# Attention with 32-row bands per head: one 1024-column exponential per key tile, and row maxima in three single PSUM banks

## The reference

```python
def _L0_xattn_ref(queries, keys, values, Wq, bq, Wk, bk, Wv, bv, Wo, bo):   # 8 heads of 4 columns
    q = _split_heads(queries @ Wq + bq)
    k = _split_heads(keys @ Wk + bk)
    v = _split_heads(values @ Wv + bv)
    scale = 1.0 / np.sqrt(D_MODEL / NUM_HEADS)
    attn = jax.nn.softmax(jnp.einsum('bhqd,bhkd->bhqk', q, k) * scale, axis=-1)
    o = jnp.einsum('bhqk,bhkd->bhqd', attn, v)
    return o.transpose(0, 2, 1, 3).reshape(b, s, h * hd) @ Wo + bo
...
x = x + jnp.tanh(g_xattn[0]) * _L0_xattn_ref(_layernorm(x), ctx_1024, ctx_1024, ...)
x = x + jnp.tanh(g_ffn[0]) * _L0_ffn_ref(_layernorm(x), ...)
```

## Time and profile before

| | |
|---|---|
| median of three runs | 595.02 us |
| the profiled execution | 594.75 us |
| its span | 592.9 us |
| PE, DVE, ACT, POOL busy | 551.4, 444.1, 397.4, 196.8 us |
| granted clock of TensorE | 1.00 until 500 us, 0.97 behind it |

### The profile page before, as it was taken

The page is one execution under the profiler, slowest core; times in us unless marked ns, Lnnn a source line. Parts: engine busy times, 40 slices in busy tenths (PEclk is TensorE's granted clock), DMA queues, the critical chain, the costliest instruction groups (busy, mean ns, idle before and its releaser), DMA issues.

```text
span 592.9 us, 12821 instructions
## 1 busy us (share of the span) xinstructions
PE 551.4 (93%) x5043; PEld 318.6 (54%) x5043; DVE 444.1 (75%) x811; ACT 397.4 (67%) x774; POOL 196.8 (33%) x193
## 2 busy tenths in 40 slices
PE   6798899998999989999999998899999999999994
PEld 4433333333333333333333344469889898898974
DVE  3889879996798967989897258746767868677541
ACT  2587789987888878898888830044665646655651
POOL 3058030024420063400158010240735626346234
PEclk9999999999999999999999999999999999999998
DMA  8600000000000000000000004122735556356133
GB/s 280 241 2 1 1 1 3 2 1 38 2 36 2 2 37 1 37 2 1 37 38 2 36 19 140 34 60 72 163 112 117 144 136 148 108 107 163 16 36 35
DMA packets 23807, 35.80 MB, mean 60 GB/s; under 512 B 3459, under 2 KB 16196, under 8 KB 23620
## 3 DMA queue, kind: packets, MB, share of 16 engines
q1 hardware_dynamic: 17604, 26.59, 13.8%
q0 software_dynamic: 6144, 8.39, 8.3%
HBM read 26.59 MB, written 8.39 MB: 59 GB/s over the span
## 4 chain that ended last, share of the span: by engine, by line
PE 67%; DVE 18%; ACT 5%; issue 4%; POOL 3%; DMA 1%; POOLq 0%; ACTq 0%; DVEq 0%; SPq 0%
PE ps L1719 15%; PE ps L1726 15%; PE ps L1488 12%; DVE mquart L1016 11%; PE ps L1475 6%; PE ps L1454 6%; PE ps L1384 2%; ACT probs L741 2%; PE ps L1345 2%; POOL xn L528 2%; PE ps L1360 1%; PE ps L1697 1%; PE ps L1672 1%; ACT osb L641 1%; PE ps L1513 1%
## 5 line engine op out<-in xcount | busy, mean ns | idle before, releaser
L1016 DVE TENSOR_REDUCE mquart<-ps 128x2 f32<-128x802 f32 x256 | 241.9, 988 | 33.4 <-PE ps L1454 30.2
L741 ACT ACTIVATE probs<-ps 128x512 f32<-128x512 f32 (+1 forms) x416 | 222.9, 599 | 24.0 <-PE ps L1475 20.8
L1488 PE MATMUL ps<-probs,vp 128*32 128x256 f32 (+1 forms) x1664 | 132.7, 391 | 4.5 <-ACT osb L641 4.5
L1454 PE MATMUL ps<-kpad,qrows 64*128 64x401 bf16 x512 | 90.6, 337 | 3.7 <-DVE mquart L1016 3.1
L1475 PE MATMUL ps<-qfull,kpad 64*128 64x256 bf16 (+1 forms) x832 | 89.8, 272 | 2.8 <-ACT x L762 0.9
L1313 DVE TENSOR_TENSOR h1l<-hf,h1h 128x512 fp32r<-128x512 f32 x64 | 44.4, 693 | 56.0 <-ACT hf L868 56.0
L867 ACT ACTIVATE h1h<-ps,b1T 128x512 fp32r<-128x512 f32 x64 | 44.0, 687 | 53.8 <-PE ps L1719 53.6
L1726 PE MATMUL ps<-w2h,h1h 128*128 128x256 f32 x256 | 73.8, 288 | 2.2 <-DVE h1l L1313 1.5
L1726 PE MATMUL ps<-w2l,h1h 128*128 128x256 f32 x256 | 72.4, 283 | 0.0
L1726 PE MATMUL ps<-w2h,h1l 128*128 128x256 f32 x256 | 72.3, 283 | 0.0
L1475 PEld LDWEIGHTS ps<-qfull,kpad 64*128 64x128 bf16 (+1 forms) x832 | 38.9, 96 | 48.2 <-ACT probs L741 25.1
(11 more groups left out here) (198 smaller groups left out, 682.3 us busy)
## 6 DMA issues: line engine op xcount, KB each, us to landing
w1raw<-in_L_ffn_w SPq DMA_DIRECT2D x16, 512.0 KB, 4.6
w2raw<-in_L_ffn_w SPq DMA_DIRECT2D x16, 512.0 KB, 4.7
xs<-in_x SPq DMA_DIRECT2D x4, 512.0 KB, 7.7
ctx_sb<-in_ctx SPq DMA_DIRECT2D x3, 512.0 KB, 5.8
out<-xs SPq DMA_DIRECT2D x3, 512.0 KB, 2.6
x_rows<-x SPq DMA_DIRECT2D x3, 512.0 KB, 2.6
b2b<-in_L_ffn_b SPq DMA_DIRECT2D x1, 1024.0 KB, 11.1
out<-xs SPq DMA_DIRECT2D x2, 256.0 KB, 2.0
```

Source lines behind the costliest of these rows:

```text
L741: nc.scalar.activation(out_p, ps[0:w, next_bank(), :], ACT.Exp, scale=float(SCALE)).then_inc(s_ex, 1)
L1016: nc.vector.tensor_reduce(mquart[:, u % 2, t, a, :, kq], ps[:, b:b + 2, 0:MAXW], AX.X, ALU.max).then_inc(s_mr, 1)
L1454: last = mm(ps[:, bank + b, 0:MAXW], qrows[band(b), g, q:q + P], kpad[band(b), g, a, lo:lo + MAXW], start=True, stop=True)
L1488: last = mm(ps[32 * hh:32 * hh + 32, PV, 0:UW], vp[0:w, kt, g, hh, :], probs[0:w, step % PROBS, hh, :], start=(kt == 0), stop=(kt == NKT - 1))
```

## The change

- **Bands.** The keys stand in `kbands`, one band of 32 partitions per head, with no zeros. A second copy, `kturned`, has its two halves of 64 partitions swapped; DMAs write it (`turn_keys` on SP's queue). The queries' lower half is copied in the same way into `qturned`. Score matmuls now contract over 32 partitions and always use bands 0 and 1 (`score_band`), maximum matmuls bands 2 and 3 (`max_band`). `qfull` has the four heads in 64 partitions and two versions. The heads take other places in a group (`place_of`), so the weights are spread in another order, with 10 copies on DVE where there were 18.
- **Exponentials.** The ring of ACT is two pairs of banks (0 and 1, 2 and 3). A step has one exponential of 1024 columns where it had two of 512.
- **Maxima.** The ring of DVE is three single banks (4, 5, 6). A maximum tile is one matmul of 401 columns for one head and one reduction of 401; a unit has 32 of them.
- **Order.** In a step PE issues the four score matmuls first, band 0, 1, 0, 1, and then all of the step's maximum tiles. Before, those of the first half step stood ahead of the scores.
- **Removed.** The multiplications with a mask that filled `kpad` (8 on DVE, L985, and 8 on ACT, L711).
- **Moved.** The loads of `b2b`, `w1raw` and `w2raw` stand on SP's queue behind the turned keys and the first turned queries, and the stores of the chunks are written out with the turned queries between them.
- `place_max` has six matmuls with 64 output partitions instead of three with 128. The copy to `qfull` has 512 columns, and the two scaled copies of the output projection are one of 1024.

```diff
-TILES = UQ * 2 * QUARTERS
+TILES = UQ * 2 * QUARTERS * 2
...
-        kpad = ar("kpad", [P, NG, 2, KEYS], BF16)
+        kbands = ar("kbands", [P, NG, KEYS], BF16)
+        kturned = ar("kturned", [P, NG, KEYS], BF16)
         vp = ar("vp", [P, NKT, NG, HG, 32])
         qrows = ar("qrows", [P, NG, S], BF16)
         xs = ar("xs", [P, QT, D])
-        qfull = ar("qfull", [P, NG, CW], BF16)
+        qturned = ar("qturned", [P, NG, 2, CW], BF16)
+        qfull = ar("qfull", [P, NG, 2, CW], BF16)
...
         def act_bank(n):
-            return n % 3
+            return 2 * (n % 2)
         def dve_bank(n):
-            return 3 + 2 * (n % 2)
-        def band(p):
-            return slice(64 * p, 64 * p + 64)
+            return 4 + n % 3
+        def score_band(p):
+            return slice(32 * p, 32 * p + 32)
+        def max_band(b):
+            return slice(64 + 32 * b, 64 + 32 * b + 32)
+        def half_tile(j):
+            a, j = divmod(j, TILES // 2)
+            return 1 - a, j // (2 * QUARTERS), j // 2 % QUARTERS, j % 2
+        def place_of(head):
+            return 2 * (head % 2) + head // 2
...
+            def turn_keys(j, g):
+                lo, w = KB[j]
+                sp.wait_ge(s_rows, BLOCKS.index(("k", j, g)) + 1)
+                sp.dma_start(kturned[64:P, g, lo:lo + w], kbands[0:64, g, lo:lo + w]).then_inc(s_kup[g], 16)
+                sp.dma_start(kturned[0:64, g, lo:lo + w], kbands[64:P, g, lo:lo + w]).then_inc(s_kdown[g], 16)
+            def turn_queries(c, g):
+                sp.wait_ge(s_rows, rows_of(c, g))
+                if c > 1:
+                    sp.wait_ge(s_mm, TILES * (PER_CHUNK * (c - 2) + PARTS * (g + 1)))
+                sp.dma_start(qturned[64:P, g, c % 2, :], qrows[0:64, g, CW * c:CW * c + CW]).then_inc(s_qt[NG * (c % 2) + g], 16)
+            for g in range(NG):
+                for j in range(4):
+                    turn_keys(j, g)
+                turn_queries(0, g)
+            sp.dma_start(b2b[:, :, :], b2.rearrange("e h -> (e h)").partition_broadcast(P)).then_inc(s_b2, 16)
             for half in range(2):
                 load_w1(0, half)
                 load_w2(0, half)
-            with sp.Fori(0, LAST) as c:
+            for g in range(NG):
+                turn_queries(1, g)
+            for c in range(LAST):
                 sp.wait_ge(s_x1, c + 1)
-                sp.dma_start(out_v[:, bass.ts(c, CT), :], xs[:, bass.ts(c, CT), :]).then_inc(s_out1, 16)
+                sp.dma_start(out_v[:, CT * c:CT * c + CT, :], xs[:, CT * c:CT * c + CT, :]).then_inc(s_out1, 16)
+                if c + 2 < NC:
+                    for g in range(NG):
+                        turn_queries(c + 2, g)
...
-            def exp(u, kt, p):
+            def exp(u, kt):
                 w = kt_rows(kt)
                 step = NKT * u + kt
-                act.wait_ge(s_sc, 2 * step + p + 1)
-                if p == 0:
-                    at_least(act, s_pv, step + 1 - PROBS)
-                out_p = probs[0:w, step % PROBS, 2 * p:2 * p + 2, :].rearrange("p h q -> p (h q)")
-                nc.scalar.activation(out_p, ps[0:w, next_bank(), :], ACT.Exp, scale=float(SCALE)).then_inc(s_ex, 1)
+                act.wait_ge(s_sc, step + 1)
+                at_least(act, s_pv, step + 1 - PROBS)
+                bank = next_bank()
+                nc.scalar.activation(probs[0:w, step % PROBS, :, :].rearrange("p h q -> p (h q)"),
+                                     ps[0:w, bank:bank + 2, :].rearrange("p b q -> p (b q)"), ACT.Exp, scale=float(SCALE)).then_inc(s_ex, 1)
...
+                take(qfull[0:64, g, :, UW * h:UW * h + UW], ps[0:64, next_bank(), :].rearrange("p (v q) -> p v q", v=2), s_qf)
...
             def keys_split(j):
                 lo, w = KB[j]
-                split(j, j % 2, w, 2, krows[:, j % 2, 0:w])
-                dve.wait_ge(s_rows, j + 1)
-                for b in range(2):
-                    last = nc.vector.tensor_scalar(kpad[:, 0, b, lo:lo + w], krows[:, j % 2, 0:w],
-                                                   cst[:, C_HEAD + b:C_HEAD + b + 1], None, ALU.mult)
-                last.then_inc(s_kpad0, 1)
+                split(j, j % 2, w, 2, kbands[:, 0, lo:lo + w])
...
-                t, a, kq = j // (2 * QUARTERS), j // QUARTERS % 2, j % QUARTERS
+                a, t, kq, b = half_tile(j)
                 dve.wait_ge(s_mm, n + 1)
-                b = next_bank()
-                nc.vector.tensor_reduce(mquart[:, u % 2, t, a, :, kq], ps[:, b:b + 2, 0:MAXW], AX.X, ALU.max).then_inc(s_mr, 1)
+                nc.vector.tensor_reduce(mquart[:, u % 2, t, a, b, kq:kq + 1], ps[:, next_bank(), 0:MAXW], AX.X, ALU.max).then_inc(s_mr, 1)
...
             def next_act(reader):
                 n = len(act_readers)
-                if n >= 3:
-                    pe.wait_ge(*act_readers[n - 3])
+                if n >= 2:
+                    pe.wait_ge(*act_readers[n - 2])
                 act_readers.append(reader)
                 return act_bank(n)
             def next_dve(reader):
                 n = len(dve_readers)
-                if n >= 2:
-                    pe.wait_ge(*dve_readers[n - 2])
+                if n >= 3:
+                    pe.wait_ge(*dve_readers[n - 3])
                 dve_readers.append(reader)
                 return dve_bank(n)
...
                 u, j = divmod(n, TILES)
                 c, g, h, r = unit(u)
-                t, a, kq = j // (2 * QUARTERS), j // QUARTERS % 2, j % QUARTERS
+                a, t, kq, b = half_tile(j)
                 if j == 0 and h == 0:
                     pe.wait_ge(s_rows, rows_of(c, g))
-                if n < 4:
-                    pe.wait_ge(s_kpad0, n + 1)
+                if n == 0:
                     pe.wait_ge(s_xf, 4)
-                if (c, g, h, j) == (0, 1, 0, 0):
-                    pe.wait_ge(s_kpad1, 4)
+                if h == 0 and j == TILES // 2:
+                    if c == 0:
+                        pe.wait_ge(s_kup[g], 64)
+                    pe.wait_ge(s_qt[NG * (c % 2) + g], 16 * (c // 2 + 1))
                 bank = next_dve((s_mr, n + 1))
-                lo, q = MAXSTEP * kq, CW * c + UW * h + P * t
-                for b in range(2):
-                    last = mm(ps[:, bank + b, 0:MAXW], qrows[band(b), g, q:q + P], kpad[band(b), g, a, lo:lo + MAXW], start=True, stop=True)
-                last.then_inc(s_mm, 1)
+                lo, q = MAXSTEP * kq, UW * h + P * t
+                rows = max_band(b)
+                queries = qrows[rows, g, CW * c + q:CW * c + q + P] if a else qturned[rows, g, c % 2, q:q + P]
+                keys = (kbands if a else kturned)[rows, g, lo:lo + MAXW]
+                mm(ps[:, bank, 0:MAXW], queries, keys, start=True, stop=True).then_inc(s_mm, 1)
             def place_max(u):
...
                 q = CW * c + UW * h
                 pe.wait_ge(s_mp, u + 1)
                 bank = next_act((s_qf, u + 1))
-                mm(ps[:, bank, 0:UW], ident_bf[:, :], qrows[:, g, q:q + UW], start=True, stop=False, skip_group_check=True)
-                for t in range(UQ):
-                    last = mm(ps[:, bank, P * t:P * t + P], mparts[:, t, :, :].rearrange("p h r -> p (h r)"), ident_bf[:, :],
-                              start=False, stop=True, skip_group_check=True)
+                for v in range(2):
+                    mm(ps[0:64, bank, UW * v:UW * v + UW], ident_bf[:, 64 * v:64 * v + 64], qrows[:, g, q:q + UW],
+                       start=(v == 0), stop=False, skip_group_check=True)
+                    for t in range(UQ):
+                        last = mm(ps[0:64, bank, UW * v + P * t:UW * v + P * t + P], mparts[:, t, 2 * v:2 * v + 2, :].rearrange("p h r -> p (h r)"),
+                                  ident_bf[:, :], start=False, stop=True, skip_group_check=True)
                 last.then_inc(s_mpl, 1)
-            def scores(u, kt, p):
+            def scores(u, kt, p, v, bank):
                 c, g, h, r = unit(u)
                 w = kt_rows(kt)
-                bank = next_act((s_ex, 2 * (NKT * u + kt) + p + 1))
-                for b in range(2):
-                    last = mm(ps[0:w, bank, UW * b:UW * b + UW], kpad[band(p), g, b, P * kt:P * kt + w],
-                              qfull[band(p), g, UW * h:UW * h + UW], start=True, stop=True)
-                last.then_inc(s_sc, 1)
+                if (c, h, kt, p, v) == (0, 0, 0, 0, 1):
+                    pe.wait_ge(s_kdown[g], 64)
+                rows = score_band(p)
+                return mm(ps[0:w, bank, UW * v:UW * v + UW], (kturned if v else kbands)[rows, g, P * kt:P * kt + w],
+                          qfull[rows, g, v, UW * h:UW * h + UW], start=True, stop=True)
+            def score_banks(u, kt):
+                return next_act((s_ex, NKT * u + kt + 1))
             def pv(u, kt):
                 c, g, h, r = unit(u)
                 w = kt_rows(kt)
                 step = NKT * u + kt
-                pe.wait_ge(s_ex, 2 * (step + 1))
```

(10 more changed lines are left out.)

123 lines of the change are left out of this document (57 added, 66 removed).

## The result

The changed kernel takes 610.68 us (median of 4, 610.26 to 611.01) against 595.15 us (594.70 to 595.86): ratio 1.0259, 95% interval 1.0242 to 1.0277. Slower, as forecast, but 8.7 us above the 602.0, above the forecast's own range of 597 to 607 and just outside the wider one of 590 to 610.

What follows compares the result with a forecast made beforehand. DVE was to set the pace in nearly every stage: 7.5 + 3.0 - 0.8 - 1.3 + 0.4 - 1.5 = +7.3 us on 594.75, forecast 602.0 us; own range 597 to 607, 8 in 10 within 590 to 610.

Steps and rivals of the forecast that it cites:

- The start: Before unit 0's maxima: dropping the mask multiplications brings the first maximum 1.3 us earlier; the reductions fit beside PE's work.
- the last unit: Unit without maxima, ACT and PE alternating: 13 x 0.07 us from wider exponentials and shorter score groups, -1.5 us.
- The reductions: On DVE: one reduction of 401 columns takes 0.492 us back to back, adding 1.2 us of work a unit.
- PE's step: On PE in the attention: 0.84 us with two maximum tiles, 1.01 with three, gaining 2.4 us a unit.
- The rival without concurrency: On PE: bands don't run side by side, the step stays at 1.1 us, 606 us; chance 0.07.
- The 0.08 us more for each pair: On PE: by the skill's figure, a score pair with a maximum pair takes 0.08 us longer, 0.8 us a unit.
- The rival of the fed DVE: On DVE: PE's freed time closes 15 us of idle time before maxima, ending at 591 us; chance 0.28.
- A unit without extras: Sign in the attention: such a unit takes about 16.5 us instead of 15.3.
- The sum over fourteen: Attention stages without unit 1's: DVE-bound +6.0, PE-bound +3.0, with projections -0.8, together +8.2 us.
- a DVE-bound stage's 1.2 us: In five stages that DVE bounds: 1.2 us of added reduction work each, besides 0.3 for `place_max`.
- the stalls behind ACT: Rival at transposes and projections: scores wait behind an exponential and maxima behind those scores, 610 us; chance 0.11.
- That the clock falls: Rival in the attention: PE pauses more, the clock halves, far beyond 620 us; chance 0.04 together with another case.

Runs made afterwards that it cites:

- f2: Kernel before with bands of 32 rows only, old order and rings, plus unread matmuls in PE's pauses, including four in the last unit: 593.92 us.
- e9: Changed kernel with the old order (first half step's maxima ahead of the scores) and added matmuls in PE's pauses: 603.93 us.
- e1_steps: Changed kernel with one added 512-column matmul behind each of the six maxima of unit 0's first two steps: 607.81 us.
- e5: Changed kernel whose reductions read only the first 200 of 401 columns, all else kept: median 587.17 us, 574.50 in one execution.
- e11: Kernel before with each reduction of 802 columns split in two of 401: 602.79 us, ratio 1.0121.
- e10: Kernel before with the new order alone, all four scores ahead of the step's maxima: 602.93 us, ratio 1.0123.
- e3: Changed kernel with banks divided otherwise: three single banks for exponentials of 512, four single banks for the maxima: median 610.08 us.
- f3: Changed kernel with three single banks for exponentials of 512, four for maxima, and added matmuls in PE's pauses: median 606.06 us.
- e6_loads: Changed kernel with the loads of b2b, w1 and w2 put back ahead of the turning DMAs on SP's queue: 610.72 us.

## Why the prediction was right and where it was wrong

**Where the time went.** Executions with a mean clock of 0.995 or more line up like this: the kernel before 595, f2 (bands alone, filled) 594, e9 (with split reductions, three single banks and one exponential a tile as well) 603.9, e1_steps (with the new order too) 607.2, and the changed kernel, with the fall of its clock, 610.7. So it's about 10 us for split and banks, 3.3 for the order and 3.4 for the clock. The added matmuls of these kernels aren't all the same, so the steps are rough. Of the 8.7 us by which the forecast was short, the clock is the largest part. The start (2.0), the rest of unit 1 (1.6) and the last unit (1.25) are others, by the table above.

**The reductions.** 0.492 us was forecast, 0.487 is measured. By the Trainium skill (VectorE: DVE Perf Modes, the section on the TRN2 errata) it would be 0.543, an estimate; the trace disagrees, by 0.056 us on 401 columns and by 0.051 on 802.

**PE's step.** Right: 0.90 against 0.84 us, and bands 0 to 3 run side by side. The rival without concurrency is out. The 0.08 us more for each pair that the prediction considered would make 1.0 us over 13 steps, not 0.8, which changes nothing.

**DVE as the bound.** Right. e5 shows it: less DVE work and nothing else took 2.6 us off a stage. The rival of the fed DVE is out as well. It wanted 15 us of idle time closed; there are 32.2 where 30.8 were, in the group of DVE's maxima of the changed kernel from 47.0 to 338.6 us:
```profile
L1033 DVE TENSOR_REDUCE mquart<-ps 128x1 f32<-128x401 f32 x480 | 239.6, 566 | 32.2 <-PE ps L1480 31.9
```

**The stages.** A unit without extras takes 16.65 us (16.5 forecast). The sum over fourteen was right (8.5 us measured, 8.2 forecast once unit 1 is taken out), the shares in it weren't. I gave all of a DVE-bound stage's 1.2 us to the split. e11 gives it 0.5 to 0.75 us in units 4, 5, 9 and 13; the rest is order and store: e10 alone adds 0.57 us to unit 4. I priced the new order at nothing but PE's gain, and had the stalls behind ACT as a rival with 0.11, as a matter of small rings. It costs 7.3 us on rings that aren't changed and 3.3 on the changed kernel, hidden in my sum under a split that was overpriced. That this rival's 610 is near the measured time is luck: 3 us of it are the clock, which it didn't have.

**The start.** I took 1.3 us for the dropped multiplications of the keys and let unit 0's reductions "fit beside PE's work". Executions of the same code reach DVE's first statistics at different times (12.04 and 12.99 us in before and e10, 11.84 and 12.90 in the changed kernel and e1_steps), so spans from there are what can be compared. From there the first maximum comes 0.81 us earlier (16.45 instead of 17.26 us) without the multiplications. But the maxima then take 18.73 us instead of 17.00. e11, with the split alone, takes 17.51, and e3, with four banks, 17.48; so 0.5 us of this is the split and 1.25 the store of three banks. The reductions didn't fit beside PE's work.

**The clock.** This is the step that failed: "Rows 2 show 1.00 throughout, with pauses of the same kind", from which the sum took nothing for the clock. They were not of the same kind. Before, PE was busy 3.40 of the 4 us from 46 on and 3.52 of the next four; after, 3.02 and then 1.37 of two, because three single maxima a step wait for DVE where nothing else is to do yet. That the clock falls was there as a rival, but at 0.04 together with another, and priced as a fall of the whole attention (beyond 620). It fell for 20 us: 3.7 us of unit 1's stage, 2.9 to 3.4 of the time (610.7 against 607.8, and 607.2 at a mean clock of 0.997). What PE must do to keep its clock isn't settled by this: f3's fill wasn't enough.

**The rest of unit 1.** The 20.29 us left in e1_steps are 3.5 above before, where 1.9 was forecast. Of these, 2.3 us are in the reductions (16.96 us from the first to the end instead of 14.67), 1.0 of it the split's work. 0.98 us is one instruction: the subtraction at L1049 takes 1.17 us instead of 0.19. POOL's turn of that stretch in the changed kernel:
```profile
47.30 1.15 POOL L406 TENSOR_TENSOR qrows<-t,c 128x512 bf16<-128x512 f32 x1 [0.89 <-ACT c L706]
```
It starts 0.03 us ahead of DVE's and ends at 48.45, and DVE's ends at 48.50. In e11 the two start at 47.62 and 47.66, and it is 1.15 us again. Before, POOL's operation started at 46.76, behind DVE's at 46.61, which took 0.19. So the later end of unit 0's maxima, in both kernels with split reductions, moved two operations into an order that the prediction had no term for. PE waited for this subtraction 0.84 us ahead of `place_max`, where it waited 0.21 before.

**The last unit.** -1.5 forecast, -0.25 measured. ACT's pace there is 0.95 us a tile (five exponentials in 4.82 us, one alone takes 1.02) against 1.00 for two of 512, so 13 x 0.05 = 0.65 us of what I reckoned at 0.9; what shortened score groups should have given didn't show.

**The DMAs.** There are 18 ahead of the loads, 9 for each group, not 9. That they cost nothing was right as far as the runs show: with the loads ahead of them the time is the same (e6_loads, 610.72 us).
